# Context gate of an adaptive-attention block with tokens as rows, its bias added by VectorE, and no transposition back

## The reference, cut to what matters

```python
ctx = causal_ema(x, tau_ctx)                                  # along the 512 tokens
gate_in = concatenate([x, ctx], axis=-1)                      # (b, t, 512)
wg = sigmoid(einsum('btc,ec->bte', gate_in, Wg) + bg)         # the context gate, (b, t, 256)
gated = x * wg
h1 = gelu(einsum('btc,hc->bth', x, Wn1) + bn1)
mod = 0.5 + sigmoid(einsum('bth,dh->btd', h1, Wn2) + bn2)     # 8 numbers a token
traces = vmap(lambda tau, m: causal_ema(gated * m[..., None], tau))(tau_raws, moveaxis(mod, -1, 0))
temporal = einsum('dbtc,dc->btc', traces, softmax(blend, axis=0))
gate = sigmoid(einsum('btc,ec->bte', temporal, Wtemp) + btemp)
soma = gelu(einsum('btc,ec->bte', x, Wsoma) + bsoma)
out = layernorm(einsum('btc,ec->bte', soma * gate, Wout)) * gamma + beta    # to the feed-forward block
```

## Time and profile before

| what | us |
|---|---|
| median of the three runs | 683.1 |
| the profiled execution | 682.62 |
| span in its profile, first to last instruction | 680.8 |
| PE (TensorE) busy | 636.1 |
| DVE (VectorE) busy | 520.1 |
| POOL (GpSimd) busy | 304.4 |
| ACT (ScalarE) busy | 300.1 |

### The profile page before, as it was taken

The page is one execution under the profiler, slowest core; times in us unless marked ns, Lnnn a source line. Parts: engine busy times, 40 slices in busy tenths (PEclk is TensorE's granted clock), DMA queues, the critical chain, the costliest instruction groups (busy, mean ns, idle before and its releaser), DMA issues.

```text
span 680.8 us, 14929 instructions
## 1 busy us (share of the span) xinstructions
PE 636.1 (93%) x5738; PEld 467.3 (69%) x5766; DVE 520.1 (76%) x1060; ACT 300.1 (44%) x629; POOL 304.4 (45%) x320
## 2 busy tenths in 40 slices
PE   5896999999999999999999999999999999989773
PEld 3675777768777777768776776777677778667341
DVE  7787568696896959687796968788695897888854
ACT  3752644454435354444535445444535434615311
POOL 1178419272634636272553726163443725144322
PEclk9899999999999999999999999999999999999776
DMA  8401413041403334051322315041332322240422
...
DMA packets 81912, 52.59 MB, mean 77 GB/s; under 512 B 59058, under 2 KB 75698, under 8 KB 81330
## 3 DMA queue, kind: packets, MB, share of 16 engines
...
...
## 4 chain that ended last, share of the span: by engine, by line
PE 81%; DVE 9%; DMA 3%; issue 3%; POOL 2%; ACT 1%; another core or an unknown queue 0%; POOLq 0%; SPq 0%; DVEq 0%; ACTq 0%
PE ps L482 73%; PE ps L485 8%; DVE CT L1032 2%; DMA B<-g_rows 1%; DVE B L906 1%; DVE EB L906 1%; DMA g_rows<-G 1%; DVE ZN L912 1%; DVE HP L906 1%; DVE FT L915 1%; DVE TP L912 1%; DMA CW<-condW 0%; POOL X L1156 0%; DMA HQ<-HP 0%
## 5 line engine op out<-in xcount | busy, mean ns | idle before, releaser
L1156 POOL TENSOR_TENSOR KP<-TH,CS 128x512 f32<-128x512 f32 x32 | 45.2, 1411 | 160.2 <-ACT TH L742 156.1
L482 PE MATMUL ps<-WQ,YT 128*128 128x512 f32 (+1 forms) x256 | 90.0, 495 | 0.9 <-ACT YT L742 0.9
L1203 POOL TENSOR_SCALAR HP<-HP,FT 128x1024 f32<-128x1024 f32 x32 | 44.8, 1401 | 99.5 <-DVE FT L909 99.5
L906 DVE TENSOR_TENSOR EB<-ps,C 128x512 f32<-128x512 f32 x128 | 79.4, 681 | 11.5 <-PE ps L482 8.7
L906 DVE TENSOR_TENSOR B<-B,BLGS 128x1024 f32<-128x1024 f32 x64 | 83.8, 1352 | 2.5 <-DMA B<-g_rows 2.5
L482 PE MATMUL ps<-X1T,W 128*128 128x256 f32 x320 | 78.2, 383 | 0.2 <-DVE CT L1032 0.2
L482 PEld LDWEIGHTS ps<-WQ,YT 128*128 128x128 f32 x256 | 48.0, 193 | 36.1 <-issue 31.5
L482 PEld LDWEIGHTS ps<-X1T,W 128*128 128x128 f32 x320 | 59.3, 190 | 8.5 <-issue 0.6
L482 PE MATMUL ps<-FW,ZQ 128*128 128x512 bf16 x228 | 55.2, 385 | 3.9 <-issue 1.6
L742 ACT ACTIVATE FH<-ps,AM 128x512 f32<-128x512 f32 x64 | 43.6, 687 | 23.5 <-PE ps L482 19.5
L742 ACT ACT_TABLE_LOAD x41 | 52.6, 1283 | 2.3 <-PEq L1297 1.6
...
## 6 DMA issues: line engine op xcount, KB each, us to landing
...
```

The source lines that it names most:

```text
L482: return e0.matmul(o, l, r, start=start, stop=stop, skip_group_check=True)
L906: return e0.tensor_tensor(o, x, y, op)
L1156: return e0.tensor_tensor(o, x, y, op)
L1203: e0.tensor_scalar(HP[:, s, :], HP[:, s, :], FT[:, s, 2:3], MAGIC, ALU.mult, ALU.add).then_inc(g["hx"], 1)
```

## The change

The gate is computed with tokens as partitions: X1T and CT of one chunk become the stationary operand and Wg the moving one. `wg` is now a job of a chunk and takes a bank for each chunk. The bias lies along the columns then; it is loaded to all partitions with the other row vectors (`bpack`, 256 columns more) and added by VectorE in a new job `wb(c)` that reads the bank and writes WGT. `wgt` is one activation of 128x512 in place on WGT. `gt` multiplies with X1 (tokens as partitions, already there) and writes G. `gtr`, `g` and their semaphores are gone. All order tables are new. The whole of the change in code, the tables cut to the periods of PE and DVE:

```diff
-for _n, _w in (("theta", 256), ("tau", 9), ("ga", 256), ("ba", 256), ("gc", 256), ("bc", 256)):
+for _n, _w in (("theta", 256), ("tau", 9), ("ga", 256), ("ba", 256), ("gc", 256), ("bc", 256), ("bg", 256)):
...
 PE_PERIOD = (
-    ("ktr", 2, 1), ("cond", 1, 1), ("qtr", 2, 1), ("ztr", 2, -5), ("mod", 1, -1), ("dn", 2, -8), ("o", 2, 0), ("ema", 2, -3),
-    ("proj", 2, 2), ("ttr", 1, -2), ("wo", 2, 0), ("e", 2, 1), ("gtr", 2, -2), ("temp", 1, -2), ("gu", 2, -6), ("o", 2, 1),
-    ("low", 1, 1), ("gu", 2, -5), ("gtr", 2, -1), ("wsum", 1, 1), ("wo", 2, 1), ("wout", 2, -4), ("wout", 2, -3), ("ktr", 2, 2),
-    ("xtr", 2, 0), ("qtr", 2, 2), ("proj", 2, 3), ("dn", 2, -7), ("xtr", 2, 1), ("gate", 1, 1), ("u", 1, -1), ("ema", 2, -2),
-    ("soma", 1, 0), ("e", 2, 2), ("h1", 1, 0), ("wg", 1, 0), ("ztr", 2, -4),
+    ("ema", 2, -4), ("h1", 1, -1), ("soma", 1, -1), ("gate", 1, 0), ("o", 2, 0), ("ema", 2, -3), ("ktr", 2, 1), ("wg", 2, -2),
+    ("dn", 2, -8), ("wg", 2, -1), ("qtr", 2, 1), ("ztr", 2, -6), ("mod", 1, -1), ("ttr", 1, -2), ("wo", 2, 0), ("e", 2, 1),
+    ("proj", 2, 2), ("gu", 2, -6), ("ztr", 2, -5), ("temp", 1, -2), ("o", 2, 1), ("low", 1, 1), ("u", 1, -1), ("wo", 2, 1),
+    ("ktr", 2, 2), ("qtr", 2, 2), ("wsum", 1, 1), ("wout", 2, -4), ("wout", 2, -3), ("gu", 2, -5), ("xtr", 2, 0), ("dn", 2, -7),
+    ("cond", 1, 2), ("proj", 2, 3), ("xtr", 2, 1), ("e", 2, 2),
 )
...
 DVE_PERIOD = (
-    ("rot", 1, 3), ("tab2", 1, -2), ("em", 2, -2), ("b4", 2, -5), ("gt", 1, -2), ("modv", 1, -2), ("fin", 2, -10), ("ae", 1, -2),
-    ("og", 2, -2), ("tab1", 1, 1), ("em", 2, -1), ("on", 2, -2), ("rq", 2, 0), ("fs", 2, -8), ("fr", 2, -8), ("sg", 1, -3),
-    ("fs", 2, -7), ("og", 2, -1), ("bn2", 1, -3), ("on", 2, -1), ("zc", 2, -6), ("zc", 2, -5), ("b4", 2, -4), ("ub", 1, -2),
-    ("ctx", 1, -1), ("wred", 1, 0), ("fin", 2, -9), ("fr", 2, -7), ("zn", 1, -3), ("rq", 2, 1), ("wsc", 1, 0), ("tab0", 1, 1),
+    ("tab2", 1, -2), ("ctx", 1, -2), ("zn", 1, -4), ("rq", 2, -1), ("tab1", 1, 1), ("fin", 2, -10), ("wb", 2, -4), ("wb", 2, -3),
+    ("modv", 1, -2), ("ae", 1, -2), ("gt", 1, -2), ("og", 2, -2), ("em", 2, -1), ("on", 2, -2), ("fs", 2, -8), ("sg", 1, -3),
+    ("rq", 2, 0), ("fr", 2, -8), ("og", 2, -1), ("tab0", 1, 1), ("ub", 1, -2), ("bn2", 1, -3), ("zc", 2, -6), ("on", 2, -1),
+    ("zc", 2, -5), ("wred", 1, 0), ("b4", 2, -4), ("fin", 2, -9), ("fs", 2, -7), ("wsc", 1, 0), ("fr", 2, -7), ("em", 2, 0),
+    ("rot", 1, 3), ("b4", 2, -3),
 )
...
-        WGT = sb("WGT", [P, 2, NT])
+        WGT = sb("WGT", [P, NJ, CH])
...
             def gw(c):
                 s = c % 2
-                e.wait_ge(a["g"], c + 1)
+                e.wait_ge(v["gt"], c // 2 + 1)
...
-            def wg(u):
-                k, tok = u // 2 % 2, slice(u % 2 * CH, u % 2 * CH + CH)
+            def wg(c):
+                u, k, cols = c // 2, c // 4 % 2, slice(c % 4 * P, (c % 4 + 1) * P)
                 e.wait_ge(v["ctx"], 2 * (u + 1))
-                e.wait_ge(*emptied("wg", u))
+                e.wait_ge(*emptied("wg", c))
                 wgw = w_("wg").rearrange("p (k n) -> p k n", k=4)
-                for o in range(2):
-                    for h in range(4):
-                        m = mm(bank("wg", u)[:, o * CH:(o + 1) * CH], wgw[:, h, o * P:(o + 1) * P],
-                               X1T[:, k, h, tok] if h < 2 else CT[:, h - 2, tok], h == 0, h == 3)
+                for h in range(4):
+                    m = mm(bank("wg", c)[:, 0:CH], X1T[:, k, h, cols] if h < 2 else CT[:, h - 2, cols], wgw[:, h, :], h == 0, h == 3)
                 m.then_inc(t["wg"], 1)
-
-            def gtr(c):
...
             def ends(u):
                 e.wait_ge(v["ae"], u + 1)
-                e.wait_ge(a["g"], 2 * u + 2)
+                e.wait_ge(v["gt"], u + 1)
...
             def wgt(u):
-                tok = slice(u % 2 * CH, u % 2 * CH + CH)
-                e.wait_ge(t["wg"], u + 1)
-                e.wait_ge(v["hb"], 1)
-                e.wait_ge(t["gtr"], 2 * u - 2)
-                for o in range(2):
-                    m = af(WGT[:, o, tok], bank("wg", u)[:, o * CH:(o + 1) * CH], ACT.Tanh, bias=HB[:, o:o + 1], scale=0.5)
-                m.then_inc(a["wgt"], 1)
+                j = 2 * (u % 2)
+                e.wait_ge(v["wb"], 2 * u + 2)
+                af(WGT[:, j:j + 2, :], WGT[:, j:j + 2, :], ACT.Tanh, scale=0.5).then_inc(a["wgt"], 1)
...
-            def gg(c):
...
+            def wb(c):
+                e.wait_ge(t["wg"], c + 1)
+                e.wait_ge(d["bgb"], 16)
+                if c > 3:
+                    e.wait_ge(v["gt"], c // 2 - 1)
+                tt(WGT[:, c % 4, :], bank("wg", c)[:, 0:CH], b_("bg"), ALU.add).then_inc(v["wb"], 1)
+
             def gt(u):
-                k, tok = u // 2 % 2, slice(u % 2 * CH, u % 2 * CH + CH)
+                b, j = u // 2, 2 * (u % 2)
                 e.wait_ge(a["wgt"], u + 1)
-                stt(WGT[:, :, tok], WGT[:, :, tok], 1.0, X1T[:, k, :, tok], ALU.add, ALU.mult).then_inc(v["gt"], 1)
+                e.wait_ge(t["u"], u - 3)
+                for s in range(2):
+                    e.wait_ge(d[f"gw{s}"], 16 * (u - 3))
+                stt(G[:, b % 2, j:j + 2, :], WGT[:, j:j + 2, :], 1.0, X1[:, b % 3, j:j + 2, :], ALU.add, ALU.mult).then_inc(v["gt"], 1)
```

More of the change, by code:

```diff
@@ L37 @@
 PE_HEAD = (
[L38 to L41, removed]
@@ L42 @@
-    ("qtr", 4), ("xtr", 2), ("proj", 5), ("xtr", 3), ("gate", 2), ("u", 0), ("ema", 0), ("soma", 1), ("e", 4), ("h1", 1), ("wsum", 2),
-    ("wg", 1),
+    ("cond", 0), ("proj", 0), ("proj", 1), ("cond", 1), ("ktr", 0), ("ktr", 1), ("qtr", 0), ("qtr", 1), ("e", 0), ("low", 0), ("e", 1),
+    ("o", 0), ("proj", 2), ("gate", 0), ("o", 1), ("low", 1), ("wo", 0), ("wo", 1), ("wsum", 0), ("qtr", 2), ("ktr", 2), ("proj", 3),
+    ("e", 2), ("wsum", 1), ("cond", 2), ("cond", 3), ("xtr", 0), ("xtr", 1), ("o", 2), ("h1", 0), ("wg", 0), ("wg", 1), ("mod", 0),
@@ L44 @@
+    ("ktr", 3), ("qtr", 3), ("wo", 2), ("gate", 1), ("e", 3), ("proj", 4), ("o", 3), ("u", 0), ("qtr", 4), ("wo", 3), ("proj", 5),
+    ("xtr", 2), ("ktr", 4), ("soma", 0), ("xtr", 3), ("e", 4), ("wsum", 2), ("low", 2),
 )
 PE_PERIOD = (
[L46 to L48 removed]
@@ L63 @@
[L63 to L66, removed]
@@ L67 @@
-    ("dn", 2, -6), ("u", 1, -1), ("soma", 1, -1), ("ztr", 2, -4), ("ztr", 2, -3), ("gu", 2, -4), ("gu", 2, -3), ("ema", 2, -2),
-    ("ema", 2, -1), ("ttr", 1, -1), ("dn", 2, -5), ("temp", 1, -1), ("wout", 2, -2), ("wout", 2, -1), ("dn", 2, -4), ("dn", 2, -3),
-    ("ztr", 2, -2), ("ztr", 2, -1), ("gu", 2, -2), ("gu", 2, -1), ("dn", 2, -2), ("dn", 2, -1),
+    ("proj", 2, -4), ("gate", 1, -3), ("o", 2, -6), ("low", 1, -2), ("ema", 2, -10), ("ema", 2, -9), ("ktr", 2, -5), ("ztr", 2, -12),
+    ("dn", 2, -14), ("qtr", 2, -5), ("wo", 2, -6), ("gu", 2, -12), ("h1", 1, -4), ("e", 2, -5), ("dn", 2, -13), ("ttr", 1, -5),
@@ new lines @@
+    ("wg", 2, -8), ("ztr", 2, -11), ("mod", 1, -4), ("wg", 2, -7), ("o", 2, -5), ("temp", 1, -5), ("wo", 2, -5), ("gu", 2, -11),
+    ("xtr", 2, -6), ("ktr", 2, -4), ("proj", 2, -3), ("xtr", 2, -5), ("cond", 1, -1), ("soma", 1, -4), ("wout", 2, -10),
+    ("wout", 2, -9), ("wg", 2, -6), ("wg", 2, -5), ("ktr", 2, -3), ("dn", 2, -12), ("qtr", 2, -4), ("h1", 1, -3), ("low", 1, -1),
+    ("u", 1, -4), ("ema", 2, -8), ("ema", 2, -7), ("gate", 1, -2), ("e", 2, -4), ("ttr", 1, -4), ("ztr", 2, -10), ("ztr", 2, -9),
@@ new lines @@
+    ("wg", 2, -3), ("mod", 1, -2), ("ztr", 2, -6), ("ktr", 2, -2), ("qtr", 2, -2), ("dn", 2, -9), ("gate", 1, -1), ("e", 2, -2),
[3 rows of a table added]
+    ("wout", 2, -4), ("wout", 2, -3), ("dn", 2, -6), ("u", 1, -1), ("ztr", 2, -4), ("ztr", 2, -3), ("soma", 1, -1), ("gu", 2, -4),
+    ("ema", 2, -2), ("gu", 2, -3), ("ema", 2, -1), ("ttr", 1, -1), ("dn", 2, -5), ("temp", 1, -1), ("wout", 2, -2), ("wout", 2, -1),
+    ("dn", 2, -4), ("dn", 2, -3), ("ztr", 2, -2), ("ztr", 2, -1), ("gu", 2, -2), ("gu", 2, -1), ("dn", 2, -2), ("dn", 2, -1),
@@ L153 @@
+    ("blg", 1, -1),
 )
 SP_TAIL = (
[8 rows of a table removed]
[8 rows of a table added]
 )
@@ L291, in build @@
                  + "".join(f" x{j}" for j in range(NJ)) + "".join(f" st{i}" for i in range(6)) + " uw blg mw0 mw1 mr0 mr1 gw0 gw1 gr0 gr1 hq0 hq1")
-        t = sems("pe", "wsum cond proj lo gate qtr ktr e smm o wo xtr h1 mod wg soma gtr u ema ttr temp wout ztr gu dn")
-        a = sems("act", "lo tg sin p2 sp tab ex yt th vg qT kT ot x1t h1 mt wgt sm g tk tt tp zq fh")
+        t = sems("pe", "wsum cond proj lo gate qtr ktr e smm o wo xtr h1 mod wg soma u ema ttr temp wout ztr gu dn")
+        a = sems("act", "lo tg sin p2 sp tab ex yt th vg qT kT ot x1t h1 mt wgt sm tk tt tp zq fh")
         v = sems("dve", "h1 eps rot red hb la1 p1 la3 la px mx wsm ws1 ws2 rq em ss og bn mv "
-                 "on ctx modv ae gt ub b4 sg bn2 mv2 z1 z2 z3 z4 z5 zm f0 hp r1 r2 r3 r4 fq fin")
+                 "on ctx modv ae wb gt ub b4 sg bn2 mv2 z1 z2 z3 z4 z5 zm f0 hp r1 r2 r3 r4 fq fin")
```

(2 more changed lines are left out.)

58 lines of the change are left out of this document (22 added, 36 removed), and 116 rows, old and new, of tables (ACT_HEAD, ACT_PERIOD, ACT_TAIL, DVE_TAIL).

## The result

The kernel after takes 678.97 us (median of 8 executions, 676.12 to 681.78), the one before beside it 682.97 us (8 executions, 681.35 to 684.57). The ratio is 0.9945, with a 95% interval of 0.9923 to 0.9968: 0.55% or 4.0 us faster. The forecast was 674.5 us, 8.5 us faster. The sign is right, but less than half of the promised gain came: the time lies outside the range of 672.5 to 678 us that belonged to the forecast itself, and inside the outer one of 668 to 684. In a later series the same kernel gave 0.9948 [0.9921, 0.9974].

A forecast was written before the change was run, and what follows sets the result against it. PE was taken to bound the steady part, the chain between engines the head and tail. From the profiled 682.6 us, 7.5 (transpositions) and 1.0 (tail) gave 674.1; runs' median 0.5 higher, so 674.5 us was said, own range 672.5 to 678.

The forecast's parts named there:

- outer one of 668 to 684: Total time: from 671.4 us less 3 us of the head up to no change with its edge.
- What bounds it: Steady part: PE, busy 93% of the span and 38.59 and 38.52 of 38.80 us a unit; head and tail: the chain between engines.
- Part 1: PE: the 64 transpositions of `gtr` go, 0.235 us a chunk, 7.5 us gained in all (bounds 7.0 and 12.2).
- The waits for `ktr`: PE, every second period: about 0.3 us of waiting before `ktr` might go, 6 x 0.3 = 1.8 us.
- Part 5: Moved steps, walked through one new period: thin but positive slack, no PE wait, cost 0 (bounds -0.3 in two periods, +0.5 a period).
- the first rival: More is gained: `ktr` waits go (1.8 us) and adjacent tail `b4` give 1.3 us, 671.4 us; chance 0.20.
- Parts 2 and 3: PE: turned `wg` matmuls cost 0; ACT: some 15 us of work saved, worth nothing in the steady part.
- Part 4: DVE: `wb` adds 32 additions of 0.42 us, 13.4 us in all, 0.84 us a unit, covered by 8 us idle.
- The rivals with DVE: DVE takes the gain back, 682.5 us, chance 0.11; or DVE becomes the bound, slower, 685.5 us, chance 0.11.
- Part 6: Tail: last unit's gate chain falls from 3.12 to 1.9 us, 1.0 us gained; adjacent last `b4` up to 1.3 more, bound only.
- The head's new order: Head, before the steady periods: the reordered jobs were taken to cost 0, bounds -3 and +3 us.
- The prediction's own sign: Head: one ending over 3 us later than before was named as showing the prediction wrong.

The follow-up runs named there:

- The old order: New computation in the job order of the kernel before: 690.31 us, ratio 1.0113; with `wgt` behind ZQ, H1 and KT on ACT: 685.41 us, 1.0045.
- the one that was tried: Changed kernel with `b4` in DVE's tail moved behind both `og` and `on`: 676.14 us, ratio 0.9926.
- head version: Changed kernel, head only: first `xtr` ahead of `cond` 2, 3, their copies ahead of `yt` 2, first scans ahead of `tab2`: 674.36 and 675.51 us.

## Why the prediction was half right

- *What bounds it, and Part 1.* Right. Each transposition costs the distance of the starts, 0.10 to 0.12 us: a pair of periods lost 1.22 us, and PE's busy time in it fell by 0.93 (77.11 to 76.18), where the earlier trace rows gave 0.94. The figure of about 275 ns in the Trainium skill ("TensorE: Matmul & The Clock Gate", section on PE-mode transpose), given there for bf16, is met by the duration (276 ns) and not by the time that doubling them adds.
- *The waits for `ktr`,* a bound of Part 5 and the first rival: the gain that this rival named came. A period is 38.19 us, 0.14 less than the transpositions explain (1.5 us over 11 periods), and PE's idle time in the pair fell from 0.49 to 0.20 us. That it was the wait for `ktr` is not shown: the only waits of 0.15 us or more in the pair before, 0.16 each, stand ahead of matmuls of `gu` (FW,ZQ).
- *Parts 2 and 3.* Right: X1T and CT groups keep 0.87 us for four records, ACT's saving is worth nothing in the steady part.
- *Part 4 and the walk of Part 5.* `wb` is 0.420 us, as taken; DVE is busy for 30.8 us a period (forecast 31.2), no slack was overrun, and doubling `wb` costs nothing. The rivals with DVE fall. The old order is slower, but for other reasons than the length of `wb`.
- *Part 6, the chain of the tail.* Right in kind: the gate takes 2.0 us (1.9 forecast), and the end of the span is 2.7 us nearer instead of 1.0 (up to 2.3 with the bound that was named). Part of that can be clock: half clock behind the last `wg` costs 8.0 us in the profile of before and 6.7 in that of after.
- *The step that failed: "The head's new order I take as 0, bounds -3 and +3 us", and with it that the tail was looked at only from the last `wg` on.* The walk was done for a period and for the last unit's chain, not for the head. There the scans begin 5.1 us later, PE waits 4.0 us for them, and the clock falls behind the wait. The prediction's own sign for it, a head that ends over 3 us later, can be read at the first `mod`: 63.13 against 58.81 us (61.17 in the second profile). Three moves in the head give 3.9 us back (4.0 over both series, interval about 2 to 6), above the bound of 3, though the interval reaches below it, and with them the version has the forecast gain, 7.2 and 8.6 us. Ahead of the last `wg` every profile of the new order has 1.9 to 3.7 us more idle PE than those of the old one. No run shows what a better order there is worth; the one that was tried gave nothing clear.
- *How the parts add up stays open.* In the profiles the periods gained 1.5 us more than was forecast and the end of the tail up to 1.7 more; the head and the stretch ahead of the last `wg` lost what the forecast did not have. What the head costs against the old one differs between executions, 4.9 us in one pair of profiles and 0.4 in the other. That the head version lands on the forecast is therefore partly luck: misses of either sign cancel in it.

The Trainium skill ("SBUF — State Buffer", section "Who interferes with whom") says that a VectorE instruction with two inputs from SBUF contends with a GpSimd one that reads SBUF, and calls the contention an exclusive lock. The prediction used it on `b4` and `gt` in the periods, where it did no harm to PE (the mean `b4` multiplication went from 1352 to 1486 ns). It bites where it was not applied: the first scans beside POOL's TENSOR_SCALARs (4.68 us for two, and 3.16 in the kernel before, against 1.38) and POOL's 0.30 us operation beside `b4`, which takes 2.22 us and ends at 605.82, 0.08 us behind the pair of `b4`. The trace agrees with it in both.
